# A gated two-layer block on one core: shared feed-forward moved out of the batch loop, last batch by halves and token tiles, three program parts joined to one

## The reference, cut to what matters

```python
# x: (8, 256, 512), ctx: (8, 256, 512)
x = x + tanh(g_xattn[0]) * retention(layernorm(x), ctx)     # mask times scores summed over all batches, 4 heads
x = x + tanh(g_ffn[0]) * ffn0(layernorm(x))                 # relu feed-forward 512-512-512, plus one expert product
x = x + tanh(g_xattn[1]) * attention(layernorm(x), ctx)     # 8 heads, scores 512 x 512 per head, over features
x = x + tanh(g_ffn[1]) * moe(layernorm(x))
def moe(x):                                                 # 2048 tokens of 512
    y_s, g_s = split(x @ w_shared_up, 2)                    # 512 -> 2 x 128
    shared = (silu(g_s) * y_s) @ w_shared_down              # 128 -> 512
    scores = sigmoid(x @ w_gate)                            # 64 experts, the best 6 per token
    ...                                                     # at most 256 tokens per expert, in token order
    return shared + sum_over_k(w_k * (silu(g_r) * v_r) @ w_down[e_k])
```

## Time and profile before

| what | value |
|---|---|
| median of 3 executions | 1215.84 us (1214.21 to 1216.09) |
| the profiled execution | 1216.23 us, span 1214.5 us |
| TensorE busy | 999.5 us (82%) |
| VectorE busy | 710.4 us (58%) |
| ScalarE, GpSimd busy | 304.1 us, 611.2 us |
| moved by transfers | 252.24 MB |

### The profile page before, as it was taken

How to read it: one execution, slowest core, us unless ns; L and a number is a source line. 1 busy time by engine, 2 the same in 40 slices (tenths; PEclk the granted TensorE clock), 3 DMA queues, 4 the chain that set the end, 5 groups by cost and what they waited for, 6 DMA issues and landing times. The chain is left out here.

```text
span 1214.5 us, 16099 instructions
## 1 busy us (share of the span) xinstructions
PE 999.5 (82%) x5966; PEld 555.0 (46%) x5966; DVE 710.4 (58%) x1241; ACT 304.1 (25%) x390; POOL 611.2 (50%) x588
## 2 busy tenths in 40 slices
PE   6947989999999999999999997554499999999000
PEld 5935645454553555545545532122355555554000
DVE  3312263668877868878778766735143443443598
ACT  2321012223124132332231332310133333333000
POOL 1100004624776777667767687797344454455100
PEclk9978889999999999999999998666699999999555
DMA  5892039478471380661401304214599999984796
GB/s 180 308 366 69 28 115 391 172 266 324 172 283 63 139 312 1 205 246 53 165 27 44 114 1 166 78 50 184 176 348 339 369 351 356 368 315 155 311 418 280
DMA packets 103833, 252.24 MB, mean 208 GB/s; under 512 B 14015, under 2 KB 14399, under 8 KB 102992
## 3 DMA queue, kind: packets, MB, share of 16 engines
q1 hardware_dynamic: 50896, 137.92, 32.0%
q10 hardware_dynamic: 31872, 62.92, 13.6%
q0 software_dynamic: 20992, 50.42, 11.0%
HBM read 125.26 MB, written 134.33 MB: 214 GB/s over the span
## 5 line engine op out<-in xcount | busy, mean ns | idle before, releaser
L1343 POOL DMA_INDIRECT y_d<-e_eo,e_ids x128 | 124.8, 975 | 131.2 <-DVE e_eo L1404 104.6
L624 POOL TENSOR_TENSOR t_psum<-t_psum,t_probs 128x512 f32<-128x512 f32 x128 | 162.8, 1303 | 50.4 <-ACT t_probs L721 47.4
L888 DVE TENSOR_REDUCE t_nmx<-quad 128x4 f32<-128x2048 f32 x64 | 146.5, 2289 | 64.3 <-PE quad L1138 64.1
L721 ACT ACTIVATE t_probs<-quad 128x2048 f32<-128x2048 f32 x64 | 120.2, 1878 | 174.1 <-PE quad L1163 174.0
L644 POOL DMA_INDIRECT xs_d<-r_norm,r_xaddr x96 | 95.6, 996 | 27.0 <-issue 26.7
L1392 DVE COPY e_xT<-e_pT 128x512 f32<-128x512 f32 x64 | 44.3, 692 | 108.3 <-PE e_pT L1449 104.2
L658 POOL DMA_INDIRECT ids_d<-r_tokk,r_addr x84 | 82.6, 984 | 42.5 <-issue 20.9
L1160 PE MATMUL quad<-b_qry,b_key 32*128 32x512 f32 x512 | 79.1, 690 | 20.7 <-ACT t_probs L721 14.2
L1449 PE MATMUL e_pT<-ident,e_xg 128*128 128x128 f32 x512 | 72.1, 285 | 22.1 <-DMA e_xg<-xs_d 20.5
L605 POOL TENSOR_TENSOR f_rstd<-f_veps,mhalf 128x2 f32<-128x2 f32 x24 | 17.0, 707 | 145.2 <-DVE f_veps L789 145.2
L1138 PE MATMUL quad<-b_key,b_qry 32*128 32x512 f32 x512 | 74.9, 655 | 18.1 <-DVE t_nmx L888 14.8
(11 more groups left out here) (185 smaller groups left out, 1619.4 us busy)
## 6 DMA issues: line engine op xcount, KB each, us to landing
xs_d<-zero ACTq DMA_DIRECT2D x32, 1024.0 KB, 7.4
e_xg<-xs_d SPq DMA_DIRECT2D x32, 1024.0 KB
y_d<-zero ACTq DMA_DIRECT2D x24, 1024.0 KB
e_xg<-y_d SPq DMA_DIRECT2D x16, 768.0 KB, 11.8
e_eo<-y_d SPq DMA_DIRECT2D x16, 768.0 KB, 11.8
a_x<-in_x SPq DMA_DIRECT2D x8, 512.0 KB, 4.6
a_cT<-in_ctxT SPq DMA_DIRECT2D x8, 512.0 KB, 3.8
v_d<-a_val SPq DMA_DIRECT2D x8, 512.0 KB, 2.7
```

Of the source, the lines that this page charges most:

```text
L624: ins = g_.tensor_tensor(psum0[:, q, :], first[:, q, :], probs[s % NP][:, q, :], ALU.add)
L721: A(probs[s % NP][:, :, :], quad[:, :, :], ACT.Exp, scale=SCALE1).then_inc(W["exp_ok"], 1)
L888: V.tensor_reduce(nmx[g][:, m, :], quad[:, :, :], axis=AX.X, op=ALU.max, negate=True).then_inc(W["mx_ok"], 1)
L1343: g_.indirect_dma_start(out=y_d, out_offset=bass.IndirectOffsetOnAxis(ap=ids[:, HC * p + n:HC * p + n + 1], axis=0), in_=eo[u][:, n, :], i ...
```

## The change

All in one change:
1. The three parts return functions, and one block runs them; waits on single semaphores take the place of the block ends. Buffers lie at fixed places in one region, PSUM is one tensor of eight banks. The first batch's loads now stand ahead of the weights.
2. `R.up`, `R.shared` and `R.down` leave the loop. The transposed norm of batches 0 to 6 is stored (`R.keep`) and read back. All up products stand at the end as `L.up0` to `L.up7`; ScalarE applies Silu, VectorE multiplies once, and the down product is done in the combine.
3. The last three steps are written out as a list (`ENDING`). Batch 7's attention goes by halves of `quad` (`L.S0a`, `L.S0b`, ...), its sums of exponentials are made by TensorE (in `L.V`), and its routing goes by token tile.
4. Rows are sent as soon as their addresses are there, ahead of the ids; `R.x/6` moves up by one step.
5. In the combine TensorE takes three of the six results and the shared down product, VectorE the other three.

```diff
-    "R.turnA": ("x4T_ok", 2, 1), "R.turnB": ("x4T_ok", 2, 2), "R.gates": ("eg_ok", 1, 1), "R.up": ("shT_ok", 1, 1),
-    "R.pos": ("pos_ok", 1, 1), "R.down0": ("acc_ok", 2, 1), "R.down1": ("acc_ok", 2, 2),
+    "L.M0": ("mrow_ok", 2, 1), "L.M1": ("mrow_ok", 2, 2), "L.V0": ("sums_ok", 2, 1), "L.V4": ("sums_ok", 2, 2),
...
         sp.dma_start(mask[:, :, :, :], io["mask"]).then_inc(mask_in, 16)
+        for u in range(2):
+            sp.wait_ge(stored[u], 2 * 16)
+        v["load_front"](sp, 0)
         weights("gate_in", "wg", "gamma", "beta")
+        weights("wo_in", "wo")
+        weights("ffn_in", "wg0", "wupT", "wdnT", "wexp")
         last = NB // 2 - 1
         for u in range(2):
             store(last, 2 * last + u, u)
...
+        def r_keep(b):
+            sp.wait_ge(W["x4T_ok"], 2 * b + 2)
+            sp.dma_start(nrT_d[b, :, :].rearrange("p (k s) -> p k s", k=KC), normRT[:, :, :]).then_inc(W["nr_kept"], 16)
...
+        def last_exps(n, h):
+            def stage(b):
...
+                act.wait_ge(W["st_mm"], 8 * b + 2 * n + h + 1)
+                A(probs[n % NP][:, 2 * h:2 * h + 2, :], quad[:, 2 * h:2 * h + 2, :], ACT.Exp, scale=SCALE1).then_inc(W["exp_ok"], 1)
+            return stage
...
+        for b in range(NB):
+            act.wait_ge(W["su_mm"], b + 1)
+            A(shT[:, b, :], quad[:, b % G, S:2 * S], ACT.Silu).then_inc(W["es_ok"], 1)
...
+        for b in range(NB):
+            dve.wait_ge(W["es_ok"], b + 1)
+            V.scalar_tensor_tensor(out=shT[:, b, :], in0=quad[:, b % G, 0:S], scalar=tg_f[:, 1:2], in1=shT[:, b, :],
+                                   op0=ALU.mult, op1=ALU.mult).then_inc(W["shT_ok"], 1)
...
+                for q in range(G):
+                    r = (g * G + q) * HD
+                    mm(pV[q * HD:(q + 1) * HD, :], cT[:, n, r:r + HD], probs[s % NP][:, q, :], start=(n == 0), stop=(n == KC - 1))
+                for q in range(G):
+                    ins = mm(z[q * HD:(q + 1) * HD, :], ones32[:, :], probs[s % NP][:, q, :], start=(n == 0), stop=(n == KC - 1))
...
+        def shared_up(c):
+            def stage(b):
...
+                since(pe, W["shT_ok"], c - G + 1)
+                by_features(quad[:, c % G, :], wsu, normRT if c == LB else nrT[c], 0).then_inc(W["su_mm"], 1)
+            return stage
...
             def load_part(j):
...
-                since(sp, part_ok, j - XB - OB + 1)
+            since(sp, (half_mm, half_ok)[h], i - (XB + OB) // 2 + 1)
...
+        for u in range(2):
+            sp.wait_ge(W[f"xscat{u}"], 16 * T * TOPK * (NB // 2))
+        sp.wait_ge(W["pv_mm"], 8 * NB)
             for p in range(XB):
                 load_rows(p)
...
+            for k in range(HALF):
+                ins = V.scalar_tensor_tensor(out=acc[:, i, :], in0=parts[u][:, k, :], scalar=comb_all[:, i, HALF + k:HALF + k + 1],
+                                             in1=acc[:, i, :], op0=ALU.mult, op1=ALU.add)
...
+            dve.wait_ge(half_ok, i + 1)
+            dve.wait_ge(half_mm, i + 1)
+            V.tensor_tensor(acc[:, i, :], acc[:, i, :], pD[i % HC][:, :], ALU.add).then_inc(part_ok, 1)
...
+            mm(pD[i % HC][:, :], shT[:, i // T, (i % T) * P:(i % T + 1) * P], wsd[:, :], start=True, stop=False)
+            pe.wait_ge(part_in[u], 16 * uses(j, XB + OB))
+            pe.wait_ge(diag_ok, i + 1)
+            for k in range(HALF):
+                last = mm(pD[i % HC][:, :], diag[i % 2][:, k, :], parts[u][:, k, :], start=False, stop=(k == HALF - 1))
```

`diag` holds the identity times a token's weight (three per tile, made by ScalarE). The first lines of `ORDER` and the end of `ENDING` (a name, a slash, the batch):

```
-F.out0+0 T.sum1a+2 T.Q7+2 F.stats+0 F.out1+0 T.V4+2 T.sum1b+2 T.S0+1 T.V5+2 F.norm+0 R.up+3 T.cT+1 T.S1+1 R.shared+3
+F.out0+0 T.sum1a+2 T.Q7+2 F.stats+0 F.out1+0 T.V4+2 T.sum1b+2 T.S0+1 T.V5+2 F.norm+0 T.cT+1 T.S1+1 F.gateA+0 T.sum1c+2 F.turnA+0 T.S2+1
...
+L.S7a/7 L.S7b/7 L.P1/7 R.hot/6 L.Q2a/7 L.Q2b/7 L.M1/7 L.Q3a/7 L.Q3b/7 R.pos/6 R.slots/6 R.places/6 R.x0/6 R.x1/6 R.x2/6 R.x3/6 L.Q4a/7
+L.Q4b/7 L.Q5a/7 L.Q5b/7 L.V2/7 L.Q6a/7 L.Q6b/7 L.A0/7 L.V3/7 L.Q7a/7 L.Q7b/7 L.V4/7 L.V5/7 L.A1/7 L.add0/7 L.V6/7 L.V7/7 L.up0/7 L.up1/7
+L.add1/7 L.stats0/7 L.stats1/7 R.send0/6 R.send1/6 R.send2/6 R.send3/6 L.norm0/7 L.norm1/7 L.turn0/7 L.turn1/7 L.gates0/7 L.gates1/7
+L.sigmoid0/7 L.sigmoid1/7 L.hot0/7 L.hot1/7 L.pos0/7 L.pos1/7 L.up2/7 L.up3/7 L.up4/7 L.up5/7 L.up6/7 L.up7/7 L.slots0/7 L.slots1/7
+L.places0/7 L.places1/7 L.rows0/7 L.rows1/7
```

More of the change, by code:

```diff
@@ L420 @@
 NP = 4
+LB = NB - 1
 RELEASES = {
@@ L961, in r_hot, with stage @@
+        def r_hot(part):
+            def stage(b):
+                each, ts, n = tiles(b, part)
+                for t in each:
                     ins = V.tensor_tensor(onehot[:, t, :, :], iota_e[:, :].unsqueeze(1).broadcast_to([P, TOPK, E1]),
@@ new lines, in r_slots, with r_places, stage @@
+            return stage
+        def r_places(part):
+            def stage(b):
+                each, ts, n = tiles(b, part)
+                fits, high, a_, b_, c_, d_, r_ = (small[:, k, ts, :] for k in range(7))
+                u = b % 2
+                V.tensor_scalar(fits, pos[:, ts, :], float(CAP), None, ALU.is_lt)
+                V.tensor_scalar(high, pos[:, ts, :], float(P), None, ALU.is_ge)
+                V.scalar_tensor_tensor(out=r_, in0=topf[:, ts, :], scalar=float(CAP), in1=pos[:, ts, :], op0=ALU.mult, op1=ALU.add)
+                link("r", V.tensor_scalar(a_, topf[:, ts, :], 2.0, None, ALU.mult))
+                link("r", V.scalar_tensor_tensor(out=c_, in0=pos[:, ts, :], scalar=float(P), in1=a_, op0=ALU.mult, op1=ALU.add))
@@ L1000, in r_places @@
-                for t in range(T):
+                if part != 1:
+                    since(dve, W[f"xscat{u}"], 16 * T * TOPK * (b // 2))
+                    since(dve, W[f"scat{u}"], 16 * T * TOPK * (b // 2))
+                V.tensor_tensor(xaddr[u][:, ts, :], r_, a_, ALU.add).then_inc(W["route_ok"], 1)
+                V.tensor_tensor(addr[u][:, ts, :], d_, a_, ALU.add)
+                link("r", V.tensor_tensor(b_, fits, top[:, ts, 0:TOPK], ALU.mult))
+                for t in each:
                     link("r", V.tensor_scalar(tokk[u][:, t, :], iota_k[:, :], tok_f[:, 0:1], None, ALU.add))
@@ new lines, in vector @@
+        for t in range(T):
+            stages[f"F.gate{'AB'[t]}"] = f_gate(t)
+            stages[f"F.x1{'ab'[t]}"] = f_res1(t)
+            stages[f"F.expert{t}"] = f_expert(t)
+            stages[f"F.down{t}"] = f_down(t)
+            stages[f"L.stats{t}"] = last_stats(t)
+            stages[f"L.norm{t}"] = last_norm(t)
+            stages[f"L.sigmoid{t}"] = r_sigmoid(t)
+            stages[f"L.hot{t}"] = r_hot(t)
+            stages[f"L.slots{t}"] = r_slots(t)
+            stages[f"L.places{t}"] = r_places(t)
@@ L1249, in experts @@
+    v.update(W=W, quad=quad, work=work, pV=pV, xg=xg, eo=eo, xT=xT, e_acc=e_acc, diag=diag, shT=shT)
+    return dict(sync=sync, gpsimd=gpsimd, scalar=scalar, vector=vector, tensor=tensor)
+def experts(nc, io, out, outer, mid, v):
     XB, OB = 4, 4
```

2382 lines of the change are left out of this document (1279 added, 1103 removed), and 2 rows, old and new, of the table RELEASES.

## The result

The changed kernel took **1196.95 us** (median of 4 runs, 1194.30 to 1199.04) beside 1215.68 (1214.21 to 1216.09) for the kernel before: ratio 0.9847, 95% interval 0.9825 to 0.9869. That is 18.7 us, not 65.5. The direction was right; the time lies 19 us above the upper end of the range.

The account below looks back on a forecast made before the run. No engine bounds throughout: TensorE bounds the loop and experts, latency the ending; transfers would bound the changed combine. Savings 12.5 + 15.2 + 31.9 + 5.9 = 65.5 us off 1216.2 gave 1151, range 1136 to 1178.

Parts of the forecast that it names:

- A, the handover: Setup to loop, at 78 us: the first F.out product starts when AT is ready, 12.5 us less.
- B, the loop: Loop steps 3 to 7: removed TensorE products save 3.05 us per step, 15.2 us together.
- C, the ending: Last batch's attention, sums, routing and sends: first load of expert rows issued 31.9 us earlier, bounds 15 and 38.
- The step that failed: Ending, scores and exponentials by halves: units cost 2.4 or 2.05 us, not about 3.6; last exponential 12.9 us earlier.
- the sums: Ending: GpSimd's 10.06 us of sums disappear; x is complete 17.8 us earlier, at 792.7.
- the routing by tile: Ending: the first tile has addresses after some 16.4 us, the second 2 us later; before, routing took 22 us.
- the block end: Ending, last row send to first load of rows: 1.8 us instead of 9.4 with a block end.
- The rival on the low clock: TensorE stays at its low clock in the combine and behind V4: slower than before, 1230 us, chance 0.04.
- the sentence on cover: Before the first expert transposes: six up products of 3.7 us lie beside routing and sends, 4.7 us of cover.
- D, the combine: Combine: transfers become the bound at 4.37 us a tile, 5.9 us less, bounds -5 and 8.
- half of it: Rival: unseen waits leave the loop 5 us and the ending 17, total 1176 us, chance 0.24.

Follow-up runs that it names:

- c2: The kernel before, unchanged, run again on a chip whose traces list no waits for an unknown releaser: 1202.57 us.
- c1: The changed kernel word for word, as control on a chip without waits for an unknown releaser: 1154.11 us beside 1203.2 for the kernel before.
- g3: g4 plus nine filler products, their results unread, in TensorE's waits of the last batch: 1147.80 us beside 1203.0 for the kernel before.
- g4: Changed kernel with shorter send runs, last ids behind the first rows, R.sigmoid/6 later, first two up banks emptied earlier: 1155.31 us beside 1203.0.
- f2: Changed kernel without the last batch's 12 id sends, so some y_d rows stay unwritten: 1180.67 us beside 1217.6 for the kernel before.
- f3: Changed kernel with the loop's run of nine sends shortened to six by moving R.x3 later: 1187.8 us beside 1217.6 for the kernel before.

## Why the prediction was right or wrong

**A, the handover: right.** 12.5 us forecast, the first F.out product at 78.81 instead of 90.65: 11.8. No weight was late: TensorE waits for no transfer between 78 and 170.

**B, the loop: right without the hold, 0.6 short of it each step with it.** 3.05 us a step were forecast. Without the hold a step went from 81.41 (c2) to 78.53 (c1), 2.9 us, and TensorE waits for S0's maxima 1.42 us, as the sum said. With it, a step went from 82.7 to 80.3:

```profile
451.27 2.05 PE L1235 MATMUL banks<-b_val,AT 128*128 128x128 f32 x16
...
531.54 2.05 PE L1235 MATMUL banks<-b_val,AT 128*128 128x128 f32 x16
```

The hold costs 1.3 us a step before and 1.8 after, where ScalarE's late f_hT pushes Q2's exponential and TensorE waits 1.67 us for it. A and B together, at the start of step 7, are 25.4 us on one chip (629.07 to 603.69) and 22.8 on the other (634.26 to 611.50); step 7, the fifth of the five steps, is taken to bring B's last 3.

**C, the ending: wrong, and it holds nearly all of the miss.** First without the hold. The load of rows came 46.0 us earlier (849.11 to 803.07) where A, B and C made 59.6. Less the 28.3 of A and B that is 17.7 for C instead of 31.9. The step that failed is "a unit costs 2.4 or 2.05 instead of about 3.6. [...] the last exponential ends about 780". From Q0 on that made 36.8 us; c1 took 50.5 (707.76 to 758.24), 13.7 more. And the kernel before, with whole quads, took 43.9 on that chip (739.37 to 783.27). Q0's first product and the last exponential, in c2 and in c1:

```profile
739.37 1.14 PE L1160 MATMUL quad<-b_qry,b_key 32*128 32x512 f32 x8 [1.49 <-DVE t_nmx L888]
781.39 1.88 ACT L721 ACTIVATE t_probs<-quad 128x2048 f32<-128x2048 f32 x1 [1.02 <-PE quad L1163]
```
```profile
707.76 2.26 PE L1333 MATMUL banks<-b_qry,b_key 32*128 32x512 f32 x6 [1.46 <-DVE t_nmx L1015]
756.30 1.94 ACT L818 ACTIVATE t_probs<-banks 128x1024 f32<-128x1024 f32 x2 [0.71 <-PE banks L1336]
```

So this stretch, which was to shrink by 10.6 us, grew by 6.6. Counted from step 7's start the last exponential ends 0.35 us later than before (154.2 and 154.55), not 12.9 earlier. All that C gained it gained behind that point, 21.0 us where the sum had 19.0: there the steps on the sums, the routing by tile and the block end were right together (from the last row send to the load 9.4 us became 1.8, as forecast).

The halves were priced by a copy at full clock and the products as if TensorE kept up. At the low clock it does not: in c1 units stand 3.7 us apart, all of it TensorE.

```profile
741.24 2.08 PE L1333 MATMUL banks<-b_qry,b_key 32*128 32x512 f32 x6 [0.23 <-ACT t_probs L818]
...
744.92 2.14 PE L1333 MATMUL banks<-b_qry,b_key 32*128 32x512 f32 x6 [0.35 <-ACT t_probs L818]
```

The clock there is 0.50 (1.2 of 2.4 GHz), from 733 to 749 as from 708 to 724; around its first fall TensorE had waited 2.71 us ahead of S4 and 1.46 ahead of Q0, around its second 1.31 ahead of S7 and 2.38 ahead of Q2. g3 shows 6 to 8 us of the 13.7 to be the clock. The rest was not taken apart: VectorE's routing of batch 6 between S7 and Q2 (2.4 us of waiting), the sums' products of V0 to V3, which now stand in this stretch on TensorE (1.7, 1.0, 1.8 and 1.0 us), and the stretches at the low clock that g3 still has. The warning stood in the trace of before, a Q product of 2.09 us where the loop has 1.14, and in the earlier trace rows with a clock of 0.78:

```profile
776.35 2.09 PE L1160 MATMUL quad<-b_qry,b_key 32*128 32x512 f32 x8 [1.82 <-ACT t_probs L721]
```

The rival on the low clock had the mechanism and priced it in the combine and behind V4, not in the units between. The Trainium skill, "TensorE: Matmul & The Clock Gate", section "HAM oscillation — how this bites in real kernels", says that bursts parted by waits for transfers start slow again each time; here the waits are for VectorE and ScalarE, and g4 (mean clock 0.63 from 700 to 745) agrees, while g3 shows the converse.

**C, the sentence on cover.** "Six of the up products (3.7 us each) lie beside the routing and the sends [...] Cover: 4.7 us." Without the hold this is right: up7 ends at 804, the transposes start at 809.6. With it, up7 ends at 851.2, and by "Without it each late microsecond counts fully" all of the 20 us counted (25.6 from load to transposes instead of 5.8). No term had the hold: I had taken GpSimd's runs of sends to occupy GpSimd alone, and did not ask what the 39.0 and 14.7 us of waits for an unknown releaser were. The kernel before has a run of 27 as well (815 to 850), but little of TensorE's work stood under it; the change put the up products there, and runs of fifteen and twelve beside the last batch's units.

**What the hold takes.** The changed kernel took 1196.95 in the first result and 1154.11 in c1, 42.8 us apart; the kernel before took 1215.68 and 1203.2, 12.5 apart. The 30 us between are the difference between 49.1 gained and 18.7. The traces say where the changed kernel loses it: 7.8 us up to step 7's start, 14.7 from there to the load, 19.1 from the load to the transposes, 0.4 behind, that is, where its waits for an unknown releaser stand. f2 and f3 gave back 15 and 8 us of it by shorter runs; that all of it is the hold is read from these places, not from a run that takes the hold away alone.

**D, the combine: right.** 5.9 forecast; from the combine's first load to the end 4.6 came with the hold (82.0 to 77.4) and 4.2 without (81.7 to 77.4). The transfers are the bound at share 1.02 and 419 GB/s with the clock at 1.00, 4.38 us a tile against 4.37. The some 358 GB/s for one core that the prediction cites from the Trainium skill, "DMA: Bandwidth & Descriptors", table of limits at the head, did not bound this kernel: one core, working alone, moved 419 GB/s over 50 us. The combine begins at the low clock (0.50 from 1116 to 1122, 1.00 from 1130 on), which costs once, not per tile, so the rival that ends slower than before failed where it was to decide.

**The rivals.** The number is nearest to "half of it" (1176, C 17 without the hold), and without the hold C was indeed 17.7; of the 14 us that it lacks the clock has 6 to 8, and the rest was not taken apart. B was not halved. No rival had the hold, and the range left out what only it could give. That c1's 1154.1 lies 3 us from the forecast 1151 is luck: the kernel before is 12.5 us faster on that chip too, and the gain is 49.1, not 65.5.

## What to carry to other kernels

A wait for "remote" or a gap put down to "issue" in the middle of equal work is a cost like any other: find what runs beside it before adding more of that, here long unbroken runs of GpSimd's indirect sends. Price every product in a stage with waits at the clock that the stage's own rows show, and where TensorE waits anyway, let it multiply something. When two kernels differ in a stretch, count it in both from one event to another: the total hid that the last batch's units had become slower. And compare a change on one chip only: the same two kernels stand 49 us apart on one and 19 on another.
